# Down and up weights built per sample on GpSimd, and applied in 64-column products on TensorE

## What is computed

```python
dg = conditions @ down_gamma          # (64, 64)
db = conditions @ down_beta           # (64, 64)
ug = conditions @ up_gamma            # (64, 256)
ub = conditions @ up_beta             # (64, 256)
w_down = down_project[None] * dg[:, None, :] + db[:, None, :]   # per sample 256 x 64
act = relu(einsum('bsd,bdh->bsh', x, w_down))
w_up = up_project[None] * ug[:, None, :] + ub[:, None, :]       # per sample 64 x 256
x0 = einsum('bsh,bhd->bsd', act, w_up) + x
```

## Time and profile before

| | |
|---|---|
| three runs | 536.25, 558.26, 559.25 us (median 558.26) |
| profiled execution, its own time | 536.95 us |
| span of the profile | 535.2 us |
| TensorE products, weight loads | 458.6 us (86%), 261.6 us (49%) |
| VectorE, ScalarE, GpSimd busy | 347.5 us (65%), 282.7 us (53%), 170.3 us (32%) |
| TensorE's share of the chain that ended last | 71% |
| mean DMA traffic | 114 GB/s, 60.99 MB |

### The profile page before, as it was taken

One profiled execution on the slowest core, in us unless ns is written; L12 is line 12 of the kernel. 1 busy time (PEld: TensorE's weight loads), 2 busy tenths in 40 slices (PEclk: granted clock), 3 DMA queues, 4 the chain that ended last, 5 costly groups with the idle time before them and its releaser, 6 DMA issues.

```text
span 535.2 us, 9331 instructions
## 1 busy us (share of the span) xinstructions
PE 458.6 (86%) x3752; PEld 261.6 (49%) x3752; DVE 347.5 (65%) x653; ACT 282.7 (53%) x421; POOL 170.3 (32%) x146
## 2 busy tenths in 40 slices
PE   3896668923799999999999999999999898849981
PEld 3674335512255456654655555565556565424541
DVE  0365547593368389749865985798389768464933
ACT  0201488362645778397657965794777397202010
POOL 3008995110212331423231323223331431162221
PEclk9999766986589999999999999999999999879887
DMA  5991700330723904372264318243813462321011
GB/s 156 344 277 43 194 1 21 94 95 14 201 80 84 275 22 142 93 222 80 84 178 138 119 54 217 89 132 77 231 39 125 98 181 82 80 82 36 1 39 39
DMA packets 68831, 60.99 MB, mean 114 GB/s; under 512 B 54006, under 2 KB 55668, under 8 KB 68404
## 3 DMA queue, kind: packets, MB, share of 16 engines
q1 hardware_dynamic: 64500, 43.86, 29.8%
q0 software_dynamic: 3712, 12.59, 7.3%
q10 hardware_dynamic: 576, 3.95, 2.0%
HBM read 39.18 MB, written 21.07 MB: 113 GB/s over the span
## 4 chain that ended last, share of the span: by engine, by line
PE 71%; DVE 11%; issue 5%; SPq 4%; ACT 3%; DMA 3%; POOL 1%; ACTq 0%; POOLq 0%; DVEq 0%
PE ph L751 17%; PE pk L730 10%; PE ph L760 6%; PE pp L713 4%; PE ph L713 4%; PE pp L871 3%; PE pp L769 3%; PE pk L751 3%; PE pp L820 2%; PE pp L854 2%; PE pk L721 2%; DVE kx L1591 2%; PE pp L744 1%; PE pk L649 1%; PE ph L649 1%
## 5 line engine op out<-in xcount | busy, mean ns | idle before, releaser
L1110 ACT ACTIVATE bd<-vc,ownrow 128x512 f32<-128x512 f32 x124 | 78.3, 709 | 0.0
L1097 ACT ACTIVATE bd<-kc,ownrow 128x512 f32<-128x512 f32 x120 | 75.6, 709 | 0.3
L448 POOL TENSOR_TENSOR demod<-demod,neghalf 128x32 f32<-128x32 f32 x8 | 43.3, 5427 | 36.6 <-DVE demod L1352 36.6
L730 PEld LDWEIGHTS pk<-bd,kc 128*32 128x32 f32 x1024 | 30.8, 121 | 17.3 <-issue 11.7
L730 PE MATMUL pk<-bd,kc 128*32 128x128 f32 x1024 | 36.1, 301 | 3.2 <-ACT bd L1097 3.2
L486 POOL TENSOR_TENSOR attnT<-attnT,style 128x1024 f32<-128x1024 f32 x6 | 11.4, 1903 | 76.6 <-DMA attnT<-av_dram 76.6
L760 PE MATMUL ph<-w,hid 128*128 128x256 f32 x128 | 34.6, 417 | 0.0
L730 PE MATMUL pk<-bd,et 128*32 128x128 f32 x1024 | 31.5, 276 | 0.0
L713 PE MATMUL pp<-ys,kwT 128*128 128x512 f32 x64 | 29.0, 595 | 2.6 <-DVE ys L1574 2.6
L730 PEld LDWEIGHTS pk<-bd,et 128*32 128x32 f32 x1024 | 27.6, 111 | 3.7 <-issue 3.2
L760 PEld LDWEIGHTS ph<-w,hid 128*128 128x128 f32 x128 | 24.5, 201 | 7.1 <-issue 4.1
(11 more groups left out here) (320 smaller groups left out, 936.2 us busy)
## 6 DMA issues: line engine op xcount, KB each, us to landing
xin<-in_x SPq DMA_DIRECT2D x8, 512.0 KB, 4.5
x_dram<-x SPq DMA_DIRECT2D x8, 512.0 KB, 2.6
k_dram<-kxb SPq DMA_DIRECT2D x16, 256.0 KB, 3.4
kt<-k_dram SPq DMA_DIRECT2D x8, 512.0 KB
v_dram<-kxb SPq DMA_DIRECT2D x8, 512.0 KB, 5.0
vt<-v_dram SPq DMA_DIRECT2D x8, 512.0 KB, 5.8
x1r<-x_dram SPq DMA_DIRECT2D x8, 512.0 KB, 3.6
av_dram<-av SPq DMA_DIRECT2D x8, 512.0 KB, 5.9
```

Source lines behind the costliest of these rows:

```text
L448: gp.tensor_tensor(q, q, neghalf[:, 0:4 * CB].rearrange("p (l a b) -> p l a b", l=2, a=2), ALU.pow).then_inc(gs_dem, 1)
L730: ins = mm(pk[32 * r:32 * r + 32, o:o + 128], weights(h, 4 * i + r)[:, 16 * pair:16 * pair + 32], bd[:, h, 8 * i + 2 * r + pair, :], start ...
L1097: fn(bd[:, h, :, 16 * b:16 * b + 16].rearrange("p (q z) x -> p q z x", z=2), kc[:, 16 * h:16 * h + 16, :].rearrange("p q (z x) -> p q z x" ...
L1110: fn(bd[:, h, :, 16 * b:16 * b + 16], vc[:, SH * h:SH * h + SH, :], ACT.Copy, scale=ownrow[:, 1, b:b + 1]).then_inc(s, 1)
```

## The change

VectorE and TensorE no longer treat beta rows and gamma factors apart from the product: the weights of each of the 8 samples of a chunk are built first, and each sample's 64 tokens are multiplied by its own weights.

- **TensorE**: down is 16 products (4 pairs of samples x 2 halves of K x 2 samples), each of 128 partitions x 64 weight columns by 64 tokens, the two samples of a pair in the two halves of the output partitions. Up is 16 products of 64 partitions x 128 weight columns by 64 tokens, the two samples on the two halves of the input partitions. The db, ub and ones products are gone.
- **VectorE**: t1, row_in, t2, row_mid, the ug product, and two of the three passes over x0 are gone; two `scalar_tensor_tensor` of 128x512 write x0. ScalarE's relu is 128x256 and stands ahead of the tanh instead of behind the second half's key blocks.
- **GpSimd**: `sample_down(c)` and `sample_up(c)`, two `tensor_tensor` of 128x1024 each, for chunks 1 to 7. sample_up(a) stands ahead of the attnT product of its step, sample_down(a + 1) behind the store of the result; those of chunk 1 stand ahead of `demodulation`.
- **SyncE**: the rows of gamma and beta of all samples go to DRAM once, and each chunk's rows are read back with a broadcast over the partitions: `down_rows` (512 KB) near the head of a step, `up_rows` (1 MB) at its end, behind a wait for the up product (`p_up`). At the start up_rows(1) stands ahead of all `late_loads`.
- **Chunk 0** goes another way: TensorE multiplies condT's columns, repeated 128 times, by gamma and beta, and VectorE builds the weights out of PSUM.
- kxb, ys and x1 are no longer tensors of their own (kx in place, xT, x0); kx and x0 wait for the DMAs that read them.

```diff
+            def down_rows(c):
+                if c > 1:
+                    after(sp, w_d, c - 1)
+                sp.dma_start(down_gb[:, :, :], down_dram[:, c * CB:c * CB + CB, :].rearrange("g b h -> g (b h)").unsqueeze(0)
+                             .to_broadcast([128, 2, CB * H0])).then_inc(d_dgb, 16)
+            def up_rows(c):
+                after(sp, p_up, c - 1)
+                for r in range(2):
...
+            sp.wait_ge(as_rows, 3)
...
+            sp.wait_ge(d_rows, 32)
+            down_rows(1)
+            for part in s_wdec:
+                sp.wait_ge(part, 16)
+            up_rows(1)
             for dst, src in late_loads:
...
+                if a is not None and 0 < a < NC - 1:
+                    down_rows(a + 1)
...
                     sp.dma_start(xin[:, :, :], t["x"][:, (a + 1) * NT:(a + 2) * NT, :]).then_inc(d_x, 16)
+                    if a > 0:
+                        up_rows(a + 1)
...
+            def sample_down(c):
+                after(gp, d_dgb, c - 1, 16)
+                after(gp, p_down, c - 1)
+                settled(gp)
+                gp.tensor_tensor(w_down[:, :, :].rearrange("p k (b h) -> p k b h", h=H0),
+                                 down_proj[:, :, :].unsqueeze(2).to_broadcast([128, 2, CB, H0]), by_sample(down_gb[:, 0, :]),
+                                 ALU.mult).then_inc(w_da, 1)
...
+            def sample_up(c):
+                after(gp, d_ugb, c - 1, 32)
...
+            sample_down(1)
+            sample_up(1)
             gp.wait_ge(vs_ss, 1)
             demodulation(0, 4)
...
+            for b in range(CB):
+                ins = mm(pk[:, 128 * b:128 * b + 128], condT[:, b:b + 1].to_broadcast([128, 128]), xnT[:, 0, 192:320],
+                         start=(b % 4 == 0), stop=(b % 4 == 3), skip_group_check=True)
+            ins.then_inc(ps_dgb, 1)
+            pe.wait_ge(as_rows, 1)
+            for i in range(CB // 2):
+                ins = mm(pp[:, 512 * i:512 * i + 512], osb[:, 0, 128 * i:128 * i + 128], hnT[:, 0, :],
+                         start=True, stop=True)
+            ins.then_inc(ps_ugb, 1)
...
-                    for k in range(2):
-                        ins = mm(P0, w_down[:, k, :], xT[:, k, :], start=(k == 0), stop=(k == 1))
+                    for i in range(4):
+                        for k in range(2):
+                            for r in range(2):
+                                q = 4 * r + i
+                                ins = mm(P0[64 * r:64 * r + 64, S * i:S * i + S], w_down[:, k, H0 * q:H0 * q + H0],
+                                         xT[:, k, S * q:S * q + S], start=(i == 0 and k == 0), stop=(i == 3 and k == 1),
+                                         skip_group_check=True)
                     ins.then_inc(p_down, 1)
...
-                    for o in range(2):
-                        mm(P23[:, 512 * o:512 * o + 512], w_up[:, 128 * o:128 * o + 128], act0, start=True, stop=True)
-                    mm(P0[64:128, :], w_up[:, D:D + H0], act0, start=True, stop=True).then_inc(p_up, 1)
+                    for i in range(4):
+                        for o in range(2):
+                            for r in range(2):
+                                z = slice(64 * r, 64 * r + 64)
+                                q = 512 * r + 256 * o + S * i
+                                ins = mm(P23[:, q:q + S], w_up[z, D * i + 128 * o:D * i + 128 * o + 128],
+                                         act0[z, S * i:S * i + S], start=(i == 0 and o == 0), stop=(i == 3 and o == 1),
+                                         skip_group_check=True)
+                    ins.then_inc(p_up, 1)
...
+                    for r in range(2):
+                        z = slice(256 * r, 256 * r + 256)
+                        stt(x0[:, :, z], xT[:, :, z], 2.0, P23[:, 512 * r:512 * r + 512].rearrange("p (o n) -> p o n", o=2),
+                            ALU.mult, ALU.add).then_inc(v_x0, 1)
```

More of the change, by code:

```diff
@@ L456, in step @@
             def step(n, a, v, d, e):
+                if a is not None and a == 1:
+                    sample_down(2)
                 if d is not None:
@@ L484, in step @@
                                           bass.IndirectOffsetOnAxis(ap=pw_now[:, 0:1], axis=0)).then_inc(d_pw[0], 16)
+                    if a is not None:
+                        sample_up(a)
                     after(gp, d_or, d, 16)
@@ L501, in step @@
                     gp.dma_start(out[:, e * NT:e * NT + NT, :], yn[:, :, :]).then_inc(d_out, 16)
+                if a is not None and 1 < a < NC - 1:
+                    sample_down(a + 1)
                 if d is not None:
@@ L625, in _ @@
             mm, tr = pe.matmul, pe.transpose
+            pe.wait_ge(s_c0, ROWS)
+            for b in range(CB):
[7 more added lines that the diff above has]
+            ins.then_inc(ps_ugb, 1)
+            mm(ph[0:B, 512:768], condT, ugam, start=True, stop=True)
+            mm(ph[0:B, 768:1024], condT, ubet, start=True, stop=True)
+            mm(ph[0:B, 0:64], condT, dgam, start=True, stop=True)
+            mm(ph[0:B, 64:128], condT, dbet, start=True, stop=True)
             pe.wait_ge(s_cond, COND)
-            mm(ph[0:H0, 0:64], dgam, condT, start=True, stop=True)
-            mm(ph[64:128, 64:128], condT, dbet, start=True, stop=True)
-            for a in range(2):
-                mm(ph[:, 128 + 64 * a:192 + 64 * a], ugam[:, 128 * a:128 * a + 128], condT, start=True, stop=True)
             for l in range(2):
@@ L778, in step @@
                     after(pe, v_kx, a - 1)
-                    turn(P23, xin, p_xT)
+                    if first(a):
+                        pe.wait_ge(s_proj, PROJ)
+                        pe.wait_ge(w_d, 1)
+                        turn(pk, xin, p_xT)
+                        first_factor(0)
+                        pe.wait_ge(w_u, 1)
+                    else:
+                        turn(P23, xin, p_xT)
                 if e is not None:
@@ L826, in step @@
                     hidden(0, hnT, p_hid, stop=True)
-                if a is not None:
-                    after(pe, v_row_in, a)
-                    settled(pe)
-                    mm(P1[0:H0, :], db_rows[64:128, :], row_in, start=True, stop=True).then_inc(p_db, 1)
-                    if first(a):
-                        first_factor(1)
                 if v is not None:
@@ L867, in step @@
                     proj(ph, owT, attnT, p_o)
-                if a is not None:
-                    after(pe, v_row_mid, a)
-                    for o in range(2):
-                        ins = mm(P01[:, 512 * o:512 * o + 512], ub_rows[64:128, 128 * o:128 * o + 128], row_mid, start=True, stop=True)
-                    ins.then_inc(p_ub, 1)
-                    if first(a):
-                        first_factor(3)
-                        demod_sums()
                 if v is not None:
@@ L1166, in step @@
                     key_blocks(0, 4, 8, a_bk0)
+                if a is not None:
+                    after(act, p_down, a)
+                    fn(act0[:, :], P0[:, 0:N // 2], ACT.Relu).then_inc(a_act0, 1)
                 if e is not None:
@@ L1480, in step @@
                     tt(hnT[:, :, :], hnT[:, :, :], halves(P01), ALU.mult).then_inc(v_hT, 1)
-                if a is not None:
-                    after(ve_, p_down, a)
-                    tt(by_batch(row_in), by_batch(P0[64:128, :]), per_batch(batch_eye[64:128, :], 64, a), ALU.mult
-                       ).then_inc(v_row_in, 1)
-                    after(ve_, a_act0, a - 1)
-                    tt(by_batch(t1), by_batch(P0[0:H0, :]), per_batch(dg[:, :], H0, a), ALU.mult).then_inc(v_t1, 1)
-                    if first(a):
-                        first_factor(0)
-                    after(ve_, p_db, a)
-                    after(ve_, v_t1, a)
-                    tt(t1, t1, P1[0:H0, :], ALU.add).then_inc(v_t2, 1)
-                    if first(a):
-                        first_factor(1)
-                        squares()
+                if a is not None and first(a):
+                    first_factor(0)
+                    first_factor(1)
+                    squares()
                 if e is not None:
@@ L1529, in step @@
                         stt(yn[:, j, :], yn[:, j, :], rstd[:, 2, j:j + 1], x2k[:, j, :], ALU.mult, ALU.add).then_inc(v_yr, 1)
-                if a is not None:
-                    after(ve_, v_up, a)
-                    stt(x0[:, :, :], xT[:, :, :], 2.0, x0[:, :, :], ALU.mult, ALU.add).then_inc(v_x0a, 1)
-                    if first(a):
-                        first_factor(2)
                 if d is not None:
@@ L1544, in step @@
                         stt(x2T[:, f, :], tmp_o[:, f, :], cols[:, 6 + f:7 + f], x1r[:, f, :], ALU.add, ALU.add).then_inc(v_x2, 1)
-                if a is not None:
-                    after(ve_, p_ub, a)
-                    after(ve_, v_x0a, a)
-                    tt(x0[:, :, :], x0[:, :, :], halves(P01), ALU.add).then_inc(v_x0, 1)
```

233 lines of the change are left out of this document (132 added, 101 removed).

## The result

| | before | after |
|---|---|---|
| median, us (4 runs of each, side by side) | 547.67 (536.25 to 559.25) | 558.61 (553.58 to 573.41) |
| ratio, 95% interval | | 1.0382 (1.0287 to 1.0477) |
| profiled execution, us; its span | 536.95; 535.2 | 553.58; 551.8 |
| mean granted TensorE clock | 0.927 | 0.902 |

The change makes the kernel 3.8% slower. It was forecast 2.6% faster. Of most kernels here some executions lose time in their first 80 us and end 8 to 23 us later; the ratios leave them out, and of a trace that comes from one (experiments 2, 3, 5, 6 and 7) only stretches behind 80 us are read.

What follows compares the result with a forecast made beforehand. TensorE was taken to bound the kernel from about 150 to 412 us. Savings of 3.3 (start), 1.5 and 0.9 (steps 1, 2) and 8.5 us (five steps) made 14.2: 522.8 us profiled, 543.5 median, range 512 to 560.

Steps and rivals of the forecast that it cites:

- A rule on the port: VectorE beside GpSimd: one traced pair was not held, though the skill's rule says two-SBUF-input operations are; no cost was forecast.
- I price these at nothing: GpSimd's four added operations a step, 9.4 us, and the waits queued behind them or SyncE's: 0 us.
- rival C: GpSimd's sample_down holds VectorE's x2: +1.8 us in each of five steps, step 2 +2.6, 543.8 us; chance 13%.
- The start: From kernel start to networks_hidden: less TensorE work, partly offset by late loads, 3.3 us saved (0 to 6).
- the start of first_factor(0) at 17.6 us: At the start: TensorE's up rows, parameters and turn of x come first, so first_factor(0) begins at 16 to 20 us.
- The late loads: At the start: SyncE issues them until 42.5 us, the last lands at 45.5, and networks_hidden would be ready at 45.4.
- B: At the start: slower TensorE rate, p_up of chunk 0 at 31 us or later, late loads 5 us late: 528 us; 17%.
- Steps 1 and 2: Step 1 gains 1.5 us by ub leaving the chain, step 2 gains 0.9 us behind the attention output.
- D: Short down and up products cost 3.8 us each, as first_factor's: +1.4 us a step, 544 us; chance 10%.
- the wait of the projection for yn: Full steps: yn was 0.35 us ahead of the output projection, so up's saving is absorbed; expected TensorE gap about 0.6 us.
- 1.8 us a step (1.7 forecast): Steps 3 to 7: 0.8 us from down and db plus 0.9 us from ub shorten each step by 1.7 us.
- A: TensorE's saved work counts in full: each full step 4.1 us shorter, 509.5 us; chance 8%.

Runs made afterwards that it cites:

- experiment 2: Kernel before plus two scratch GpSimd operations of 128x1024 ahead of the attnT product, where the changed kernel has sample_up: ratio 1.0109.
- experiment 3: Kernel before plus five GpSimd memsets of 128x1024 at sample_down's place, which write SBUF and read nothing: ratio 0.9997.
- experiment 5: Changed kernel with sample_down(a + 1) moved from beside x2 to right behind sample_up(a): ratio 1.0050 to the kernel before.
- experiment 6: Changed kernel with only sample_up(2) moved one step earlier, behind sample_down(2): lowest time 550.22 us against 553.58, no interval.
- experiment 7: Changed kernel with sample_up(2) one step earlier and, from step 3 on, sample_down right behind sample_up: ratio 0.9947 to the kernel before.
- experiment 1: Kernel before plus two scratch GpSimd operations of 128x1024, two inputs each, at sample_down's place beside x2 in steps 2 to 6: ratio 1.0354.
- experiment 4: Kernel before plus one scratch GpSimd product of 2.4 us at sample_down's place in five steps: ratio 1.0078.
- Experiment 10: Experiment 7's kernel with w_dec loads issued behind the conditioning loads, ScalarE's copy of the conditioning ahead of that wait: ratio 0.9821 to the kernel before.
- experiment 11: Experiment 10's kernel with sample_up(1) behind the first of GpSimd's four powers: ratio 0.9869 to the kernel before.
- experiment 9: Experiment 7's kernel with w_dec loads and ScalarE's conditioning copy behind the conditioning loads, sample_up(1) behind GpSimd's first power: ratio 0.9971 to the kernel before.

## Why the prediction was wrong

The step that failed is **"A rule on the port"**, and with it the sentence "I price these at nothing" under GpSimd. sample_down is not free beside x2: in place of nothing it cost 4.9 us a step, 3.1 of VectorE held and 1.8 of clock.

- *Rows 8 were the wrong witness.* I set rival C at 13% "against: rows 8". That pair was a one-input operation of GpSimd over 24 partitions and an addition over 5. The prediction said that it tells little, and still let it speak against the rule. The Trainium skill, "SBUF — State Buffer", section "Who interferes with whom", says what the runs then showed: a VectorE instruction with two SBUF inputs is blocked by a GpSimd one that reads SBUF (x2 4.53 us, experiment 1), not by one that only writes (1.42 us, experiment 3), and one with a single SBUF input is not (1.22 us for the one that begins inside sample_up). It excepts modes that a cast, among others, can enter, and experiment 5 bears that out (2.72 us). Why rows 8 show no hold stays open; by the page's rule they should. The changed kernel has the same pair, and it is not held there either (1.21 us at 109.60, inside GpSimd's operation from 108.34 on).
- *C was priced too low.* It had +1.8 us a step; measured from before to after it is +3.1, and from the kernel without the hold (experiment 5, 48.2 us) to the changed one +4.9. The hold itself was rather over-priced: C put the turn of x2T at 307.4 where the forecast had 303.9, 3.5 us, and 3.1 were measured. What C lacked is the clock: the other 1.8 us of the 4.9 lie behind the turn of x2T, and experiments 1 and 4 show 1.6 us of this kind by themselves. C also counted five steps and step 2 beside x2; it is four, since step 7 has no sample_down and x2 of step 2 kept its 1.42 us (159.41).
- *C was missed altogether in step 2.* The prediction looked for VectorE's partners only at x2, and not for those of sample_up, which runs "while GpSimd would wait anyway": 4.1 us.
- *The start*: forecast -3.3 us, measured +3.4. The term that failed is the start of first_factor(0) at 17.6 us. It was built from TensorE's records alone; that the w_dec loads, released 6 us earlier, would make cols and kaffT late (12.2 and 10.6 us to land, against 1.9 and 2.2) was not asked. Experiment 10 brought first_factor(0) to 15.85 us, but the turn of x of step 1 only to 62.40, and experiment 11 to 61.88: 2.1 and 2.6 of the 3.4 us (64.50 in the changed kernel, 61.13 before). The late loads were forecast to land at 45.5, by a load of 2.6 us; the last of them took 8.98 us and landed at 54.48. B had the late loads right; its reason for them was not what happened. TensorE's rows for up took 3.87 us, the short end of the forecast, and p_up of chunk 0 came at 33.6 us because cols was late.
- *Steps 1 and 2*, forecast -2.4 us, measured +2.7: the 4.1 us of the table parts, less 1.4 that did come (step 1 alone gave 0.2 of its 1.5).
- *What held*: down 1.08 and up 1.96 us (1.1 and 2.3 forecast; D is out), the wait of the projection for yn (0.78 us; its slack before was 0.2 us within the timeline, 297.15 to 297.33, not 0.35), of the turn for x2 (0.88), and 1.8 us a step (1.7 forecast), which steps 3 to 6 show as soon as GpSimd's work stands elsewhere, and step 7 in the changed kernel itself. A, 4.1 us a step, did not come in any run.

The sum on the profiled executions: start +3.4, steps 1 and 2 +2.7, four periods +12.5, step 7 -1.7, together 16.9 in rounded terms; the spans differ by 16.6. Against the forecast of 522.8 us it is 30.8 us more: four times 4.9 and 4.1 for GpSimd's holds with their clock (23.7), 6.7 for the start, and 1.0 that steps 1 and 2 were to give and did not. That is 31.4; the full steps gave 0.3 more than forecast without the hold, and 0.3 is rest.

## What to carry to other kernels

Of GpSimd's work that reads SBUF, the operations of 128x1024 here were free only where VectorE had nothing with two SBUF inputs, and no cast, beside them: before moving it, list VectorE's operations in that window, in every step in which the place differs, and look where their operands lie. If a hold cannot be avoided, keep it short: one that left TensorE a wait under 1 us cost only itself here, one of 3 to 4 us cost half as much again in clock. And where loads are put in another order, follow what each wait releases on the other queues: with 3.9 MB that start 6 us earlier, 7 KB took 10 us longer to land.

## What the runs showed of the hardware that I had not expected

- A wait of TensorE of 2.84 to 3.99 us was followed by some 3 to 4 us of work at 1.2 GHz (granted clock 0.50 in the window behind it); one of 0.77 us was not. Between them the length does not decide alone: behind 2.60 us the k projection ran at 3.70 us in the kernel before and at 6.45 in experiment 9. What TensorE did further back differs there, and I did not take that apart.
- A hold lasts until GpSimd's operation is over, whatever the size of the one held: an addition of one partition by 256 elements, 0.42 us alone, took 2.44.
- Two GpSimd operations 0.07 to 0.08 us apart hold two passes one after the other. VectorE's pass seems to get in between and to hold GpSimd in turn: GpSimd's second operation took 2.69 us against 2.36. This reading is not shown by a run of its own.
- A cast from fp32 to bf16 with one SBUF input was held like the additions (2.72 us, 0.68 alone).
